# Full attention layers in another order beside the causal layers, and causal score matmuls of 512 columns

## The chip, the cores and the metric

The kernel runs on one NeuronCore of one Trainium2 chip. The metric is the device time of one execution in microseconds; below, "time" is the median over several executions. TensorE is called PE, its weight loads PEld, VectorE DVE, ScalarE ACT, GpSimd POOL, SyncE SP.

## What is computed

Four layers follow each other on a batch of B = 4 images with C = 256 channels and N = 32 x 32 = 1024 positions, all in float32:

```python
x = L0(x)   # q, k of 32 channels, v of 256; softmax(q k) v; gamma * out + x
x = L1(x)   # group norm; q, k, v of 256 channels; softmax(q k / 16) v; wo; + x
x = L2(x)   # causal: layer norm, 8 heads of 32 with one common k and v,
            # softmax(causal(q k)) v, wo; layer norm; feed-forward with
            # two layer norms and gelu; tokens x channels
x = L3(x)   # as L1, with weights of its own
```

L0, L1 and L3 are full attention: for each image 1024 x 1024 scores, a softmax over a row and the product with the values. L2 is causal multi-query attention over the same 1024 positions, with a feed-forward part behind it. Images don't depend on each other; in one image the layers do.

## The kernel before

**Two streams.** All work is cut into pieces. One stream, the full stream (`full_chain`), runs the twelve full layers (a layer on an image, as L1.3 for layer L1 on image 3) one after the other in the order of the list `FULL` (line 35). The other, the causal stream (`causal_chain`), runs the causal layer L2 on image 0, 1, 2, 3, named C0 to C3. A string for each engine (`ORDER`, line 43) says from which stream its next piece comes: `weave` (line 270) takes one character after the other and lets that stream emit one piece. For PE the character is also the PSUM bank at which the piece's output begins (0 to 7 for the full stream, a to h for the causal), F and C where a piece opens no new output. There are 1317 PE pieces, 690 of ACT, 868 of DVE, 128 of POOL and 66 of SP. All is fixed when the kernel is built; at run time engines wait for each other by semaphores, and each works through its pieces in order.

**Full layer.** `full_events` (line 97) lists its PE pieces: group norm means `gn` (L1, L3), queries `q`, values `v`, then for each of eight tiles of 128 positions the scores `s` (two steps of 512 keys), transposes of the normalised probabilities `t` (two steps), and for each quarter of the positions the value product `o` (four steps of eight matmuls, line 732). A full layer has 54 (L0) or 56 steps. ACT takes the exponent (line 1036) and copies transposes (1049); DVE takes row maxima, scales and adds the residual.

**Causal layer.** An image has 162 PE steps. For each of K = 8 blocks (a group of four heads by a quarter of 256 queries) there are `max` steps (`causal_max`, line 933: scores queries x keys, from which DVE takes the row maximum, line 1565), a `shift` step that turns the maxima, `exp` steps (`causal_exponents`, line 951: scores keys x queries, for the tile jt of 128 keys, with the shift as two more rows of the contraction; ACT takes the exponent, line 1205) and `values` steps (line 978). The queries of four heads lie in `qs` [128, 2, 4, 512]: four slices of 512 columns. Outputs for the four heads stand side by side in one or two banks of 512 columns (`heads`, line 545; `width` says how many banks). Then come, for each quarter, `wo`, layer norms, `ta`, `w1`, `tg`, `w2`, each of which needs the one before it. In `max` the causal mask of a diagonal tile is added by a bf16 matmul of 128 columns (line 948) right after each score matmul (line 946). In `exp` each head is a matmul of its own (line 959), with the same stationary operand:

```python
for a in range(4):
    last = mm(heads(name)[:, a, 0:n], ks[0:3 * DH + 2, jt * P:(jt + 1) * P],
              stack(k, a, 3 * DH + 2, QUARTER - n, QUARTER), start=True, stop=True)
```

n is 256 queries, or 128 for the second tile on the diagonal; of the 160 `exp` steps of the kernel 128 have n = 256 and 32 have n = 128.

**Buffers.** `home` (line 369) says where a layer's image lies: L0 and L1 in x[b % 2], L3 in z (image 3: in x[0]). x[0] and x[1] are loaded by SP once the causal layer has read their former image. The output of L2 goes to L3's home; as z is used for three images in turn, PE waits (in `stage`, kind w2) for the stores of the image before to be done. Group norm statistics of L3 have one buffer. SP carries all DMAs in order: the x loads, the stores of L3's results (`stores`, line 579), the copies that build `qs` (`stacks`, 586) and those of the shifts (`shifts`, 601).

Of the kernel before, what the change touches and what calls it, by code (L numbers as in the profile page):

```python
# [34 lines left out]
FULL = [("L0", 0), ("L1", 0), ("L0", 1), ("L1", 1), ("L0", 2), ("L3", 0), ("L1", 2), ("L0", 3), ("L3", 1), ("L1", 3),  # L35
# [14 lines left out]
        "FhdFbCFfd0chF6e23e0b2FFF630FFF6aCCeCgC1adfFdCfd3bC3fa2aFhe5aFc0cC52hfa2CFhC560FcfC725Fahca7C23eaFgcFeFag4CFa"  # L50
        "g360heCF37C6eFCFaCFhC3fF017fC5dC6FaFhFcf4C6aC2FdFFeCaC2F4gCFC0Cc3fF0F62FCe015F723Fab025FFghF3F60Cbb3F576FaFF"
        "2F745ag0b2FFF37geha6hFhFFceagc3eahcea6Fc3adf6a3FfCga2FhefC0cheC5c3a5caFC4c3a5aFdC27fab3Fhf6h05bCcFaCFceFagC2"
        "eaFge5a62ahF567FFF2F01567FFF320FFF5hCCbCdC5hacFaCcaaCcaaehc5aeC20FgfcCeC0fcCegcFeCcgeabgdCfb135hdCCbCeC6bCFf"
        "43bC6FeCb3e01gFfC3g0C6fFbCFaFChC5CFCh3c40F5Cg72FFF3Fa1256h4FFdaF12Cf7FFFda25dhF02e5F0F2hega4h4g0F2df7dfabd5F"
# [21 lines left out]
    "POOL": (
        "FCCCCCCCCCCCCCCFCCCCCCCCCCCCCCCCCCFCCCCCCCCCCCFCCCCCCCCCCCCCCCCCCCCCFCCCCCCCCCFCCCCCCCCCCCCCCCCCCFCCCCCCCCCC"
        "CCCCCCCCCCCCCCCCCCCF"),
    "SP": (
        "FCCCCCCCCCCCCCCFCCCCCCCCCFCCCFCCCCCCCCCCCCCCFFCCCCCCCCCCCFCCCCFCFF"),  # L80
# [1585 lines left out]
```

## Time and profile before

| what | value |
|---|---|
| time, median of 3 executions | 1485.58 us (1484.95 to 1488.01) |
| the profiled execution, its own time | 1486.03 us |
| its span, first to last instruction | 1484.2 us |
| instructions | 22513, of them 9152 matmuls and as many weight loads |
| mean granted TensorE clock | 0.958 of full speed |
| DMA | 27.09 MB, 18 GB/s |

The profile tells for each engine how long it was busy, and for each group of instructions (a line of the kernel, an operation, a tile) how often and how long one ran, and what ended the idle time before it. A matmul's duration reaches from its start to the modelled end of its pipeline; matmuls overlap, so the pace of a series is the distance of their starts. The granted clock is the share of its full speed that TensorE was given; it has two levels, 1.2 and 2.4 GHz (0.5 and 1).

### The profile page before, as it was taken

What the parts mean: (1) busy time and instruction counts of PE and PEld (TensorE: products, weight loads), DVE (VectorE), ACT (ScalarE), POOL (GpSimd) and SP (SyncE); (2) the same over time, 40 slices, a digit from 0 to 9 for tenths busy, and PEclk for the clock granted to TensorE, in tenths of its full rate; (3) what the DMA queues carried; (4) which work ended last, traced back from release to release, by engine and by line L of the source; (5) the groups of instructions that cost most, each with busy time, mean ns of one, the idle gap of its engine ahead of it and who ended that gap; (6) DMA issues with size and microseconds to landing.
All of it is one profiled execution on the core that took longest, in us unless ns stands there. A gap on an engine that the chain in (4) does not pass through costs nothing.

```text
span 1484.2 us, 22513 instructions
## 1 busy us (share of the span) xinstructions
PE 1338.0 (90%) x9152; PEld 1067.9 (72%) x9152; DVE 870.6 (59%) x1854; ACT 595.3 (40%) x973; POOL 92.5 (6%) x134
## 2 busy tenths in 40 slices
PE   5889989999999899989997899988999899998498
PEld 5768766777778777767776777776678777765486
DVE  3634466776458567557456657727656667675442
ACT  3523334344355343435334534423544443444142
POOL 0000000000000000000000000000010001001000
PEclk9999989999999899999998999997999999999699
DMA  5000010000000200010000010010000100100000
GB/s 176 1 1 0 29 43 23 1 23 2 1 1 2 70 11 14 22 29 1 2 1 0 6 38 23 2 49 3 1 2 1 43 2 23 37 16 1 0 1 29
DMA packets 20613, 27.09 MB, mean 18 GB/s; under 512 B 3488, under 2 KB 14240, under 8 KB 20512
## 3 DMA queue, kind: packets, MB, share of 16 engines
q1 hardware_dynamic: 20512, 25.66, 6.2%
q8 instruction: 74, 1.21, 0.3%
q14 instruction: 27, 0.22, 0.1%
HBM read 8.61 MB, written 4.19 MB: 9 GB/s over the span
## 4 chain that ended last, share of the span: by engine, by line
PE 79%; DVE 9%; ACT 6%; issue 2%; DMA 1%; SPq 1%; POOL 0%; ACTq 0%; DVEq 0%
PE ring L679 27%; PE ring L732 22%; PE ring L978 9%; PE ring L946 5%; PE ring L959 5%; PE ring L723 4%; ACT probs L1036 2%; PE ring L760 1%; PE ring L881 1%; ACT probsT L1049 1%; ACT cprobs L1205 1%; PE ring L948 1%; PE ring L916 1%; DVE part_max L1565 1%; SPq L595 1%
## 5 line engine op out<-in xcount | busy, mean ns | idle before, releaser
L732 PE MATMUL ring<-probsT,vt 128*128 128x256 f32 x1536 | 358.5, 387 | 16.7 <-ACT probsT L1049 16.4
L732 PEld LDWEIGHTS ring<-probsT,vt 128*128 128x128 f32 x1536 | 288.6, 193 | 67.4 <-ACT probsT L1049 20.6
L1205 ACT ACTIVATE cprobs<-ring 128x1024 f32<-128x1024 f32 (+1 forms) x160 | 150.4, 942 | 247.6 <-PE ring L959 246.9
L1036 ACT ACTIVATE probs<-ring,neg_max 128x1024 f32<-128x1024 f32 x96 | 107.1, 1116 | 185.4 <-DVE neg_max L1282 87.7
L1565 DVE TENSOR_REDUCE part_max<-ring 128x2 f32<-128x1024 f32 (+2 forms) x112 | 127.2, 1143 | 47.6 <-PE ring L946 34.2
L946 PE MATMUL ring<-ks,qs 96*128 96x512 f32 (+3 forms) x384 | 129.8, 421 | 16.4 <-ACT cprobs L1205 3.7
L1049 ACT COPY probsT<-ring 128x512 f32<-128x512 f32 x192 | 102.3, 592 | 48.2 <-PE ring L723 48.2
L959 PE MATMUL ring<-qs,ks 98*128 98x256 f32 (+1 forms) x640 | 114.5, 302 | 5.8 <-ACT probs L1036 1.4
L1281 DVE TENSOR_REDUCE shift_max<-ring 128x1 f32<-128x1024 f32 x64 | 78.3, 1224 | 70.3 <-PE ring L679 68.4
L723 PE MATMUL ring<-consts,probs 128*128 128x128 f32 x768 | 106.7, 279 | 13.1 <-ACT probs L1036 7.3
L959 PEld LDWEIGHTS ring<-qs,ks 98*128 98x128 f32 x640 | 91.4, 192 | 27.4 <-issue 15.6
L723 PEld LDWEIGHTS ring<-consts,probs 128*128 128x128 f32 x768 | 88.0, 143 | 32.1 <-ACT probs L1036 8.5
L679 PE MATMUL ring<-h_hi,q_hi 128*128 128x512 f32 x256 | 106.5, 416 | 3.6 <-ACT probs L1036 3.2
L946 PEld LDWEIGHTS ring<-ks,qs 96*128 96x128 f32 x384 | 77.4, 211 | 34.6 <-issue 10.4
L679 PE MATMUL ring<-h_hi,q_lo 128*128 128x512 f32 x256 | 100.5, 392 | 0.0
L679 PE MATMUL ring<-h_lo,q_hi 128*128 128x512 f32 x256 | 100.2, 392 | 0.0
L978 PE MATMUL ring<-cprobs,v 128*32 128x256 f32 (+1 forms) x1280 | 96.9, 375 | 0.0
L978 PE MATMUL ring<-cprobs,ones 128*32 128x256 f32 (+1 forms) x1280 | 92.9, 362 | 0.0
L643 POOL TENSOR_TENSOR rstd<-var_eps,half_neg 128x2 f32<-128x2 f32 (+1 forms) x56 | 44.8, 801 | 538.2 <-DVE var_eps L1463 538.2
L658 POOL TENSOR_SCALAR_AFFINE_SELECT cprobs<-cprobs 128x512 f32<-128x512 f32 x64 | 41.9, 657 | 540.6 <-ACT cprobs L1205 540.5
L1293 DVE TENSOR_SCALAR probs<-probs,row_inv 128x1024 f32<-128x1024 f32 x96 | 72.4, 754 | 3.4
L679 PEld LDWEIGHTS ring<-h_hi,q_hi 128*128 128x128 f32 x256 | 48.2, 188 | 19.9 <-issue 7.9
(215 smaller groups left out, 2212.1 us busy)
## 6 DMA issues: line engine op xcount, KB each, us to landing
x<-x_dram SPq DMA_DIRECT2D x4, 1024.0 KB, 6.5
qs<-q_hi SPq DMA_DIRECT2D x32, 128.0 KB, 2.3
qs<-q_hi SPq DMA_DIRECT2D x64, 64.0 KB, 2.0
out_dram<-z SPq DMA_DIRECT2D x6, 512.0 KB, 2.8
qs<-q_lo SPq DMA_DIRECT2D x16, 128.0 KB, 2.3
qs<-max_rows SPq DMA_DIRECT2D x128, 2.0 KB
qs<-q_lo SPq DMA_DIRECT2D x32, 64.0 KB, 2.0
out_dram<-x SPq DMA_DIRECT2D x2, 512.0 KB, 2.8
```

The source lines that it names most:

```text
L679: ins = mm(out, w, m, start=first and n == 0, stop=last and n == len(every) - 1)
L723: last = nc.tensor.transpose(o[:, j, :], probs[:, ti % 2, (TPH * hf + j) * P:(TPH * hf + j + 1) * P], ident)
L732: last = mm(o[:, ct * QUARTER:(ct + 1) * QUARTER], vt[:, j, ct * P:(ct + 1) * P], probsT[:, qi % (NQ - 1), j, :], start=j == 0, stop=j == ...
L946: last = mm(o, stack(k, a, 3 * DH, at, at + P), ks[0:3 * DH, lo:hi], start=True, stop=not diag)
L959: last = mm(heads(name)[:, a, 0:n], ks[0:3 * DH + 2, jt * P:(jt + 1) * P], stack(k, a, 3 * DH + 2, QUARTER - n, QUARTER), start=True, stop ...
L978: last = mm(acc[DH * a:DH * (a + 1), (half + 1) * QUARTER - n:(half + 1) * QUARTER], w, causal_probs(step, n)[:, a, :], start=jt == 0 and ...
L1036: A(probs[:, ti % 2, :], flat(full_name(l, b, ("s", ti))), ACT.Exp, bias=neg_max[:, ti:ti + 1], accum_out=row_sum[:, ti:ti + 1]).then_inc( ...
L1049: nc.scalar.copy(probsT[:, ti // 2 % (NQ - 1), js, (ti % 2) * P:(ti % 2 + 1) * P], slot(name)[:, 0, :].rearrange("p (s n) -> p s n", n=P)) ...
L1205: A(causal_probs(step, n), heads(name)[:, :, 0:n], ACT.Exp).then_inc(read_done["c", "act"], 1)
L1281: full_then(v.tensor_reduce(shift_max[:, ti:ti + 1], flat(name), AX_X, ALU.max, negate=True))
L1293: v.tensor_scalar(probs[:, ti % 2, :], probs[:, ti % 2, :], row_inv[:, ti:ti + 1], None, ALU.mult).then_inc(probs_scaled["dve"], 1)
L1565: v.tensor_reduce(cols if ti < TPH else parts[:, ch, :], src[:, :, 0:n], AX_X, ALU.max, negate=True).then_inc(read_done["c", "dve"], 1)
```

## The change

Three things. (1) In `FULL`, L1.3 stands before L3.1. (2) All five order strings are new; the numbers of pieces are the same. (3) In `causal_exponents` a matmul takes all heads that share a bank: two of 256 columns or four of 128; in `causal_max` the masks come after all scores of the tile, and only the first matmul of a bank has start=True, only the last stop=True.

With them, `home` gives L3.1 the buffer x[1], L3.2 x[0], L3.3 z, and L0.3 z; the x load of L0.3 moves behind the stores of L3.0 on SP and waits for them to be done; PE's wait for the stores goes; L3's statistics have two buffers.

```diff
-FULL = [("L0", 0), ("L1", 0), ("L0", 1), ("L1", 1), ("L0", 2), ("L3", 0), ("L1", 2), ("L0", 3), ("L3", 1), ("L1", 3),
+FULL = [("L0", 0), ("L1", 0), ("L0", 1), ("L1", 1), ("L0", 2), ("L3", 0), ("L1", 2), ("L0", 3), ("L1", 3), ("L3", 1),
         ("L3", 2), ("L3", 3)]
...
     "PE": (
-        "0F2eF60F2Fe50F72d5F401F756FFF3F750F62d7FFF0F6572d4FFF017FFF05F204F6F2046F012F405F710FFF2F456F012FFF3Ff70120F"
+        "0Fc4F60F2Fe50F72d5F401F760FFF3F516F021FFF3F0215ga1FFF027FFF03F513F5F0246F012F405F710FFF2F456F012FFF3F5670b3F"
...
     "SP": (
-        "FCCCCCCCCCCCCCCFCCCCCCCCCFCCCFCCCCCCCCCCCCCCFFCCCCCCCCCCCFCCCCFCFF"),
+        "FCCCCCCCCCCCCCCCCCCCCCCCCCCFCFFCCCCCCCCCCCCCCCCCCCCCCCFCCCFCCCFFFF"),
...
+        def gn_stats(l, b):
+            return all_stats[l][:, b % 2 if l == "L3" else 0, :, :, :]
+
         def home(l, b):
-            return x[b % 2] if l != "L3" else x[0] if b == B - 1 else z
+            return (z, x[1], x[0], z)[b] if l == "L3" else (x[0], x[1], x[0], z)[b]
...
             def full_chain():
-                for b in range(2, B):
-                    wait_filled(sp, f"C{b - 2}.xt1")
-                    sp.dma_start(home("L0", b)[:, :, :], x_dram[b]).then_inc(x_in[b % 2], 16)
-                    yield
-                for b in range(B):
+                wait_filled(sp, "C0.xt1")
+                sp.dma_start(home("L0", 2)[:, :, :], x_dram[2]).then_inc(x_in[0], 16)
+                yield
+                yield from stores(0)
+                sp.wait_ge(y_out, 16 * NB)
+                sp.dma_start(home("L0", 3)[:, :, :], x_dram[3]).then_inc(x_in[1], 16)
+                yield
+                for b in range(1, B):
                     yield from stores(b)
...
                 elif kind == "w2":
-                    if 0 < b < B - 1 and hf == 0:
-                        pe.wait_ge(y_out, 16 * NB * b)
...
-                for i in range(4) if two == 2 else range(2):
-                    o = heads(name)[:, i, 0:hi - lo] if two == 2 else slot(name)[:, i, 0:hi - lo]
+                own = 4 // width[name] if two == 2 else 1
+                outs = [(heads(name) if two == 2 else slot(name))[:, i, 0:hi - lo] for i in range(4 if two == 2 else 2)]
+                for i, o in enumerate(outs):
                     a = i if two == 2 else 2 * two + i
-                    last = mm(o, stack(k, a, 3 * DH, at, at + P), ks[0:3 * DH, lo:hi], start=True, stop=not diag)
-                    if diag:
-                        last = mm(o[:, hi - lo - P:hi - lo], mask[:, 0, :], mask[:, 1, :], start=False, stop=True)
+                    last = mm(o, stack(k, a, 3 * DH, at, at + P), ks[0:3 * DH, lo:hi], start=i % own == 0,
+                              stop=not diag and i % own == own - 1)
+                if diag:
+                    for i, o in enumerate(outs):
+                        last = mm(o[:, hi - lo - P:hi - lo], mask[:, 0, :], mask[:, 1, :], start=False,
+                                  stop=i % own == own - 1)
...
-                for a in range(4):
-                    last = mm(heads(name)[:, a, 0:n], ks[0:3 * DH + 2, jt * P:(jt + 1) * P],
-                              stack(k, a, 3 * DH + 2, QUARTER - n, QUARTER), start=True, stop=True)
+                own = 4 // width[name]
+                for a in range(0, 4, own):
+                    last = mm(heads(name)[:, a:a + own, 0:n], ks[0:3 * DH + 2, jt * P:(jt + 1) * P],
+                              stack(k, slice(a, a + own), 3 * DH + 2, QUARTER - n, QUARTER), start=True, stop=True)
```

What the new strings do, counted from the PE string (first and last step of each layer among the 1317):

| layer | before | changed |
|---|---|---|
| C0 | 101 to 425 | 105 to 402 |
| L0.1, L1.1 | 118 to 235, 246 to 366 | 118 to 230, 239 to 379 |
| C1 | 426 to 744 | 403 to 714 |
| L0.2, L3.0, L1.2 | 371 to 446, 447 to 569, 570 to 697 | 382 to 465, 473 to 603, 607 to 713 |
| C2 | 745 to 1038 | 715 to 991 |
| L0.3 | 702 to 780 | 717 to 821 |
| L3.1 | 786 to 897 | 983 to 1114 |
| L1.3 | 898 to 1043 | 841 to 981 |
| C3 | 1039 to 1260 | 992 to 1260 |
| L3.2 | 1046 to 1202 | 1123 to 1259 |
| L3.3 | 1261 to 1316 | 1261 to 1316 |

In the last steps of C3 (`tg2`, `w22`, `wo3`, `ta3`, `w13`, `tg3`, `w23`) no step of a full layer stands between them before. Changed, L3.2's `t10` to `t13` and two `o` steps stand between `wo3` and `ta3`, two `o` steps between `ta3` and `w13`, `t14`, `t15` and two `o` steps between `w13` and `tg3`, and two `o` steps between the two halves of `w23`.

## Rows read from the trace of the kernel before

**Rows 1.** The profile page: busy time of each engine, and the chain that ended last.
```profile
PE 1338.0 (90%) x9152; PEld 1067.9 (72%) x9152; DVE 870.6 (59%) x1854; ACT 595.3 (40%) x973; POOL 92.5 (6%) x134
...
PE 79%; DVE 9%; ACT 6%; issue 2%; DMA 1%; SPq 1%; POOL 0%; ACTq 0%; DVEq 0%
```

**Rows 2.** Windows: us, then busy us (x instructions) by engine, granted PE clock, DMA.
```profile
149.40:478.50 329.10, 308.63 (x2183) 244.63 (x2182) 210.31 (x431) 143.06 (x225) 22.16 (x31) 0.97 0.06 14
478.50:827.60 349.10, 320.95 (x2224) 255.54 (x2223) 209.85 (x446) 143.11 (x230) 22.83 (x32) 0.96 0.06 16
827.60:1150.40 322.80, 298.24 (x2087) 233.90 (x2086) 195.90 (x429) 132.01 (x216) 23.61 (x32) 0.96 0.06 14
1150.40:1321.90 171.50, 159.28 (x1150) 125.22 (x1149) 116.16 (x250) 68.74 (x112) 14.98 (x21) 0.98 0.09 23
1321.90:1402.10 80.20, 55.87 (x508) 40.20 (x506) 42.93 (x108) 28.15 (x40) 7.19 (x10) 0.83 0.02 8
```

**Rows 3.** Waits of PE from 1321.9 to 1402.1 us: total, times, longest.
```profile
PE ring L881 <- DVE an L1479: 12.2, 3, 6.9
PE ring L679 <- DVE act_lo L1544: 4.0, 2, 3.4
PE ring L902 <- DVE max_cols L1576: 3.0, 1, 3.0
```

**Rows 4.** PE in order of time before L3.3: start, us; idle before in brackets.
```profile
1385.37 1.11 PE L881 MATMUL ring<-consts,an 128*128 128x128 f32 x4 [6.88 <-DVE an L1479]
...
1387.90 0.58 PE L679 MATMUL ring<-ffw_hi,hn_hi 128*128 128x256 f32 x1 [1.41 <-DVE hn_lo L1249]
...
1394.43 1.11 PE L881 MATMUL ring<-consts,an 128*128 128x128 f32 x4 [3.61 <-DVE an L1479]
...
1402.13 0.39 PE L750 MATMUL ring<-gn_in,consts 128*128 128x4 f32 x2 [2.60 <-DVE gn_in L1326]
...
1406.12 0.77 PE L760 MATMUL ring<-h_hi,L_wqk_hi 128*128 128x512 f32 x1 [3.60 <-issue]
```

**Rows 5.** PE in order of time: scores in fours, and a value step.
```profile
1239.86 1.09 PE L946 MATMUL ring<-ks,qs 96*128 96x512 f32 x4
...
705.93 1.89 PE L732 MATMUL ring<-probsT,vt 128*128 128x256 f32 x8
```

**Rows 6.** Groups by form: busy us, mean ns of one; idle before.
```profile
L959 PE MATMUL ring<-qs,ks 98*128 98x256 f32 x512 | 93.7, 306 | 5.7 <-ACT probs L1036 1.4 <-DMA qs<-max_rows 1.4 <-DVE part_max L1565 1.1
L959 PE MATMUL ring<-qs,ks 98*128 98x128 f32 x128 | 20.8, 285 | 0.1
L959 PEld LDWEIGHTS ring<-qs,ks 98*128 98x128 f32 x640 | 91.4, 192 | 27.4 <-issue 15.6 <-DVE part_max L1565 1.8 <-DMA qs<-max_rows 1.6
L948 PEld LDWEIGHTS ring<-mask 128*128 128x128 bf16 x256 | 26.5, 104 | 21.6 <-issue 9.0
L679 PE MATMUL ring<-h_hi,q_lo 128*128 128x512 f32 x256 | 100.5, 392 | 0.0
...
ACT cprobs L1205 <- PE ring L959: 246.9, 112, 8.3
```

**Rows 7.** PE in order of time: score and mask by turns, 384 and 512 columns.
```profile
1202.37 0.44 PE L946 MATMUL ring<-ks,qs 96*128 96x384 f32 x1 [1.29 <-DVE h_lo L1249]
...
1202.69 0.42 PE L946 MATMUL ring<-ks,qs 96*128 96x384 f32 x1
...
1203.47 0.45 PE L946 MATMUL ring<-ks,qs 96*128 96x512 f32 x1
...
1203.80 0.47 PE L946 MATMUL ring<-ks,qs 96*128 96x512 f32 x1
```

**Rows 8.** Waits of PE over the span, and DMA issues (to landing).
```profile
PE ring L916 <- DMA out_dram<-z: 3.3, 2, 1.7
...
x<-x_dram SPq DMA_DIRECT2D x4, 1024.0 KB, 6.5
...
out_dram<-z SPq DMA_DIRECT2D x6, 512.0 KB, 2.8
```

More of the change, by code:

```diff
@@ L50 @@
[L50 to L54, printed above, removed]
@@ new lines @@
+        "FF457FFFac4F6F0ce5F0F2h4F670F234gFahc601hFaFF4cgacFg7a6c0F457gcFcaefFcaFf1F3705gCgbegbCdhaC6fbdFaCfFcaFcCe76"
+        "h6aFfFhabCceCbFhdfCbgda6fb1F3hfCC1dC6fCFb2eFgeC6bddC1fa3ahc5dFa7dC05hbFd7C03bCFfa7C56dhaFdCFadFahfc0cCFec624"
+        "dFdCC6a23CeCFgCFaFbC3fCFac75a6d4C7aCFgFdCFaC76fC3CFCeFcFCa6F3F15F3Fh0c5F730FecCfd725F017FdFF5F20db3Fh156FFF2"
+        "F701efec70bFhFFfcaeh67c6aFFhecaheFcaeaCbg0hgcCehaC1adFf3dCa5dfdC1F5dFh0ceh5c0dC4gFaC360Feh36ehC4aFgc0b67ecFF"
+        "agCFC4cCFa7C62aF04f7fFcCeFcFcCe6acFef0123g4acFCgFhFa2C4dC4FgaFCFcga4gCca4F6ca6e1gFdC5Fbd3hfC1C3gC1dFC76f3CFb"
@@ new lines @@
+        "275FdCb7C34acFfhFCFaC3fF7a6C0FdC576aCFCCFhfF1FCa34706FhFFh017FgfFFCca6F4F2a6F4F2ah4F620Fd764F076bcaeFhFhF1F0"
+        "7dfdfbca4F76da2aedgFaeFfF0F7eCcf34cf6aCchaC5FFgbdFaCg2d2adC2FfhFaFdedcCfaCecgaCebgdea2hgCCe0FC6cC4a6beFaC4aF"
+        "ggCe0cgef6ca6aC2Fega74C0gCFc74cC2aeFgaC4g5a6cheFacCFeaF2egCCaFCeC60b4CgFc6C01eCcgFeFhCcCFa4bCFaCh3C72C0Cbf7F"
+        "FFCg707FFFg7a3Fcb53Cfc0F4F6c04ch0Fc345F701F340fgbcFFbFh4F0cg1cgeca5Fhcace7aca10fFFhCdbF4agbCFahgC6320be6ceCa"
+        "bFdbCFFdha52dhgaC7ebCdaFbfCdFafcdaFgfCCdChC0bf3Fa5aC5d0fFdC5Facch0ge2ac4C0hcF75dCcC3F750Fc475cCaeFcaCFcageca"
@@ new lines @@
+        "gCaFc6F23abCCaCfChCacCfCahc4F601cCdCafCcCaCFCCagFF4FCh63271FaFFa760FbcFFC74F026F4F0264F012F704F617FFF2F014F6"
+        "73FFF0F27657FFF017FFF"),
+    "ACT": (
+        "FFFFCFFFFFCCFFFCCFFFCCFFFFFFFFFFFFFFCCFFFFFFFFFFFFFFFFFFFFFFFFFFFFFFFFCFFFFCCFFFCCFFFFFFFFFFFFCCCCCFFFCCFFFC"
+        "CCCFCCFFFFCCCCCCCFFCCCCCCCCCCFFFFCCFCCFCFFCCFCFCCFFFCCFFFCCFFFCCCCCCCFFFCCFFFCCCCCCFFFFFCCCCCFFFFCCCCFFFCFFF"
+        "CFFFCCCFFFFFFCCCFFFFFFFFFFFCCCCCFFCCCCCCCCFFCCCCCFFFCCFCFFCCFFCCFFFCCFFFCCFFFCCCCCFFFCFFFCCCCFFFFFCCCFFCCCCC"
+        "FFCFFFCFCFFCCFFCCFFFCFFFCCCFFFCCCCCFFFCFFFCCCCFFFFFCFFFFCCCCFFFCFFFCCFFFFFFFFFCCCCFFFCCCFFFCCCCCCFFFCCCCFFCF"
+        "CFCCCCCCCCCCCCCFFCFFCFCFCFCFCCFCFCCFFFCCFFFCCCFFFCCCCCCCFFCFCFFFCCCCCCCCCFFFFFCCCFFCFFFCFFCCCFCFFFFCCFFFFFFF"
+        "FFCCCCFFFCCCCCFFFCCCCCCCCFFFCFFCCCCFCFCCCCCCCCCCCCFFFFFCCFCFCFFCFCCFFFCFFFCFFFCCCCCCCCFCCCFFCCCCCFFCFCCCCCCC"
+        "FFFFFCFFCCFFFFFFFFFFFFFFFFFFFFFFFFFFFFFFFF"),
@@ new lines @@
+    "DVE": (
+        "CFFFFCFFFFFFCCFFCCFFCCCFFFFFFFFFFFCCFFFFFFFFFFFFFFFFFFFFFFFFFFFFFFCCCFFFFCCFCCFCCFFFCFFFFCFFCCCFFFFCCCCCFFFC"
+        "CCCFCFFFCCCCCCCCCCCCCCCCCFCCCCCFCCCCCCCCFCFFCFCFCFFCCCFFCCFCCCFCFCCCCCFCCCFCCCCFCCCFCFCFCFCFCCCCFCCCCCCCFFFC"
+        "FCFCCCCCFCCCFCCCCCFCCCCFFFCCCCFCCCFCFFCFCCFCFCFFCCCFFCCCFCCFFFCCFCFFFFFCCCCFFFCCCCCCCCCCFFFFCFCCCCCCCFFCFCCC"
+        "CCCCFCCCCFCFCFFCCCCCCFCFFCFCCFCFCCFCCCFCFFCFCCCFCCCCCFCCCCFCCFCCCCCFCCCFFCFCFCFFFCFCCCCFCCFCFFFCFFFCCFCFCCCF"
+        "CCCCCFCFCFCFFCCCCFFCCCCFCCCCCFCCCCFFFCCCFCCCFCCFFFFCCFCFFFFFCCCCFFFCCCCCFFFCCCCCFFFCCCCCFCCCCCCCCCCCCFCCCCCF"
+        "FCCCCCCCCCCFCFCCCCFFCFFFCFCCCCCCFCCFFCCCCCFCCCCCCFCFCFCFCFCFCCCFCCCCCCCFCFFCFCCFCCCCCCCCFCCCFFCCCCFCCCCCCCCF"
+        "FCFFCCFCFFFCCCCFCCCFCCFFFCCFCFFFFCFCCCFFCCCCCFFCCCCFCCFCCCCCCCFCCCFCCCCCCCCCCCFCCCCCCCCCCCCCCCFFCCFCFCFFCFCF"
+        "CCCCCFCCFCCFCCFCCCCFCFCFCFFFFCCCCCCCCCCCCFFCFCCCCCCFCCCCCFCCCCCCCFFCCCCFCCCCCFCCCCFCFFFFFFFFFFFFFFFFFFFFFFFF"
@@ L75 @@
         "FFFF"),
     "POOL": (
[L77 to L78 removed]
+        "FCCCCCCCCCCCCCFCCCCCCCCCCCCCCCCCCCCCCCFCCCCCCCCCCCCCCFCCCCCCCCCCCCCCCCCCCCCCCFCCCCCCCCCCCCCCCCFCCCCCCCCCCCCC"
+        "CCCFCCCCCCCCCCCCCCCF"),
     "SP": (
[L80 removed]
+        "FCCCCCCCCCCCCCCCCCCCCCCCCCCFCFFCCCCCCCCCCCCCCCCCCCCCCCFCCCFCCCFFFF"),
```

33 lines of the change are left out of this document (5 added, 28 removed).

## The prediction, made before the changed kernel was run

> **What bounds the kernel now.** I read the page first, then the busy time by stage, then the waits and the order of time where the stages differ. The page shows a kernel that is bound by TensorE: PE is busy in 90% of the span and carries 79% of the chain that ended last; the other engines stand at 59% and below [rows 1]. So two things can shorten it: less time on PE for the same work, and fewer holes in PE's stream. The windows say where the holes are [rows 2]. Each of the first three causal images (149.4 to 478.5, 478.5 to 827.6, 827.6 to 1150.4 us) keeps PE busy for 308.6 of 329.1, 320.9 of 349.1 and 298.2 of 322.8 us: 94, 92 and 92%. The last causal image runs at 93% (159.3 of 171.5 us) while the full layer L3.2 runs beside it. When L3.2 has ended, at 1321.9 us, 80.2 us follow in which the causal image is alone; there PE is busy for only 55.9 us and its granted clock is 0.83 of full speed, where 0.98 was granted just before. PE waits in that stretch for the layer norms of the feed-forward part: 12.2 us in three waits for the normalised rows `an`, 4.0 for `act_lo`, 3.0 for `max_cols` [rows 3]. In order of time one sees the last pieces hand over serially: a gap of 6.88 us, one of 1.41, one of 3.61, then 2.60 and 3.60 us at the group norm of L3.3 [rows 4].
>
> **Cover for the lonely tail.** Steps of PE, counted in the order string: before, the last causal image has 162 steps of its own and 60 of full layers beside it, the last of which stands 58 steps ahead of the image's end. Changed, L1.3 comes before L3.1, so that image 3 of the causal layer starts with L3.1 and L3.2 both still to do: 107 full steps beside it, and L3.2's last value step is the second last step of the stage. Between the causal pieces `wo3`, `ta3`, `w13`, `tg3`, `w23` now stand transposes and value products of L3.2 (six, two, four and two steps in a row; a value step is eight matmuls in 1.89 us [rows 5]), which is about what the gaps of rows 4 last. Price: PE's 55.9 busy us were done at clock 0.83; at 0.98 they are 55.9 x 0.83/0.98 = 47.3, and at the 93% busy of the stretch before, 50.9 us. The 80.2 us become 50.9: **29.3 us gained**. The gaps of 2.60 and 3.60 us at the end stay: L3.3's group norm still needs the last `w2`, and nothing is left to cover it.
>
> **The cover is taken from somewhere.** The other three images have 163, 157 and 132 full steps beside them and will have 136, 150 and 115. Does a stage with fewer full steps run thinner? The rows say hardly: the stretch 1150.4 to 1321.9, with 60 full steps for 104 causal ones, is as dense (93%) as the first image with one full step per causal step (94%). I take 5 us for it, half a point of busy share on the 1001 us of those stages; bounds 0 and 29, the latter if all that the tail lost turns up again.
>
> **Exponent matmuls merged.** For 256 queries the four matmuls of 256 columns become two of 512, for 128 queries four become one of 512. 512 matmuls of 256 columns were busy 93.7 us in 128 groups of four, 732 ns a group; with a mean of 306 ns for one, their starts are (732-306)/3 = 142 ns apart. For 128 columns: 20.8 us in 32 groups, 650 ns, starts (650-285)/3 = 122 ns apart [rows 6]. Matmuls of 512 columns of the same kind, four in 1.09 us whose last takes some 0.39 [rows 5, 6], start (1.09-0.39)/3 = 233 ns apart. So a large piece goes from 4 x 142 = 568 to 467 ns, 128 times: 12.9 us; a small one from 4 x 122 = 488 to 233 ns, 32 times: 8.2 us. Together **21 us of PE**. The multiplied columns are the same: what goes are 352 of the 640 weight loads of 192 ns [rows 6], of which matmuls of 256 columns (half of 233 ns, 117) leave 25 ns each in sight, and short ones more.
> The Trainium skill ("TensorE: Matmul & The Clock Gate", "Back-to-back issue gap" and "Step-by-step") speaks against this part: it has the isolated gap as N/2.4 + 2.5 ns and lets the next weight load be pulled under the matmul in flight, by which a large piece would gain 5 ns and nearly the whole 21 us would not be there, while the 142 ns of this trace say otherwise. The measurement decides for me.
>
> **Score matmuls for the maximum.** Same count, but the masks come after all scores of a tile instead of after each. A score of 512 columns and its mask start 330 ns apart from the next pair, one of 384 columns 320 ns [rows 7]; streaming alone is 233 + 58 and 175 + 58 (scaled from the 233). There are 256 pairs. The lower bound is zero, if a mask behind a mask takes its 104 ns of weight load [rows 6]: 233 + 104 is no less than 330. The upper bound is some 65 ns a pair, 16 us. I take 5, nearer to the load's row.
>
> **What of this reaches the end.** PE is in order and 90% busy; a gain ahead of a wait is swallowed by it. Of 21 + 5 us I count nine tenths: **23.4 us**.
>
> **Buffers and queues.** The output of the causal image 1 now goes to the second x buffer instead of z, and PE's wait for the stores ahead of `w2` goes away: 3.3 us in two waits [rows 8], **3.3 us gained**. In its place SyncE waits for L3.0's two stores before it loads x for L0.3. That load takes 6.5 us and a store 2.8 [rows 8]; it is issued about 115 PE steps ahead of L0.3's first matmul (1317 steps in 1484 us, so over 120 us): hidden. If it weren't, its 9.3 us would show once at L0.3's start. Behind that wait on SyncE stand the copy of the last shift of image 1 (`shift7`, whose transposes come 26 PE steps, nearly 30 us, later), then image 2: hidden too. The doubled statistics buffer, and GpSimd's order with the same 128 steps, cost nothing: same instructions, on engines at 59% and 6%. What cover there is goes with PE's backlog; without it the group norm's chain on DVE and GpSimd would show, 6.2 us a layer as at L3.3 [rows 4].
>
> **Sum.** The profiled execution took 1486.0 us, its span 1484.2. 1486.0 - 29.3 + 5 - 23.4 - 3.3 = 1435.0. That run lies 0.4 us above the median of the three; I leave it at **1435 us**. Its own range is 1416 (masks at 16, merges in full, nothing lost from the other stages) to 1449.
>
> **Rivals.**
> *Merges swallowed* (0.16): PE's saved time ends in waits that end on ACT or DVE, or the weight loads were hidden anyway. For it: ACT waited for the exponent scores for 246.9 us in all [rows 8], so it is not the bound there, but 15% of the chain that ended last is DVE's and ACT's [rows 1]. Against: 90% busy and 142 ns. Then 1435 + 23.4 = 1458 us. The rule of the Trainium skill's page on TensorE quoted above would come out here too.
> *The holes move* (0.17): the three earlier images, with 51 full steps fewer, open the holes that closed at the end. For it: 24.3 us of idle PE over 58 lonely steps is 0.4 us a step, and 51 steps make 21 us. Against: the density of rows 2. Then the 29.3 come back in place of the 5: 1459 us. Both together (0.03) is 1483 us, no change.
> *Slower* (0.05): the merged matmul reads two or four head slices that lie 512 columns apart; if such a moving operand streamed at half rate, 512 columns would take 467 ns, a large piece 933, so 128 x 365 = 46.7 us more instead of 12.9 less, and the small ones 0.7 less instead of 8.2. 1435 + 19 (the gain missing) + 41.4 (nine tenths of 46.0) = 1495 us. It decides from about 420 ns a matmul. No row shows such an operand on PE; none hints at a cost either.
> *Not what it says* (0.01 of the above): the words speak of four full layers left; by the list three are left behind L1.3, of which two run beside the causal image and L3.3 after it. I reckon with the two.
>
> **Numbers.** Forecast 0.59, merges swallowed 0.16, holes move 0.17, both 0.03, slower 0.05. What a measurement of this kernel can tell is about 0.2%, 3 us. Faster 0.92, same 0.03, slower 0.05. The range runs from 1416, where all bounds meet, to 1467, past both middle rivals; what it leaves out is the slower case, the two rivals together, and a little on either side.
>
> **What would show it.** Right: `L959` with 288 matmuls and starts 233 ns apart, some 9,150 - 352 = 8,800 matmuls; PE's busy time down by 20 us or more beyond what the clock gives; the last 80 us ahead of L3.3's group norm over 90% busy at a clock above 0.95; no wait of PE on stores; gaps only at the last group norm. Wrong: a busy share under 90% in the first three images (holes moved); ACT's or DVE's waits at those images up by as much as PE's work went down (swallowed); matmuls of `L959` 400 ns apart (slower).

## The result, and the profile after

| | before | changed |
|---|---|---|
| time, median | 1485.26 us (1484.59 to 1488.01, 4 runs) | **1416.6 us** (1414.86 to 1420.27, 4 runs) |
| ratio | | **0.9538**, 95% interval 0.9514 to 0.9561 |
| profiled execution, its span | 1486.03, 1484.2 us | 1414.86, 1413.1 us |
| mean granted TensorE clock | 0.958 | 0.973 |

The change took 68.7 us; 51 were forecast (1435 us). The time lies at the low end of the range. Times below are medians over executions; one of e1's ten executions (2067.94 us, mean clock 0.602) and one of e3's five (1727.27 us, 0.735) are left out, and with them the medians would be 1483.2 and 1478.7 us, the latter being the figure from which the expectations of e6 and e9 start. The page of the changed kernel, busy time and chain, against [rows 1], and the merged group from its section 5 (busy us, mean ns):

```profile
PE 1303.7 (92%) x8800; PEld 1018.9 (72%) x8800; DVE 866.2 (61%) x1854; ACT 594.1 (42%) x973; POOL 93.9 (7%) x134
...
PE 82%; DVE 7%; ACT 7%; issue 2%; SPq 1%; DMA 1%; POOL 0%; ACTq 0%; DVEq 0%
...
L968 PE MATMUL ring<-qs,ks 98*128 98x512 f32 x288 | 106.6, 442 | 4.9 <-DVE h_lo L1258 2.4
```

The counts are those of the forecast: 8800 matmuls, 288 of them merged. PE's busy time fell by 34.3 us. The idle part of the span (span less busy) fell from 146 to 109 us. The matmul edits account for some 14 us of the 34.3 (e1 and e2 below). The rest goes with the clock: by the mean clocks of the table PE stood at half clock for about 125 us before (2 x (1 - 0.958) x 1484.2) and 76 after. A matmul of 512 columns starts 0.43 us behind the one before it at half clock (L3.3's queries, 1335.25 to 1335.68 us) and 0.23 at full, so this is worth at most 24 us, an estimate from those two rows. e4 below, with the new order and the old matmuls, shows it by itself: the same 9152 matmuls, busy for 19.6 us less than before, at a mean clock of 0.972.

```profile
PE 1318.4 (93%) x9152; PEld 1055.7 (74%) x9152; DVE 867.5 (61%) x1854; ACT 594.3 (42%) x973; POOL 94.2 (7%) x134
```

So three kinds of gain are there: fewer holes, more of the span at full clock, and less work on PE.

The windows of the changed kernel, for the same five stages as [rows 2] (us, then busy us by engine, clock, DMA); the last is that of the last 58 causal steps, up to L3.3:

```profile
148.90:456.20 307.30, 283.77 (x1976) 217.49 (x1975) 195.00 (x408) 134.97 (x209) 21.96 (x31) 0.97 0.06 15
456.20:775.80 319.60, 302.72 (x2091) 235.13 (x2090) 203.84 (x443) 137.30 (x227) 22.93 (x32) 0.99 0.07 18
775.80:1054.90 279.10, 259.10 (x1854) 196.28 (x1853) 189.77 (x412) 122.33 (x196) 24.33 (x32) 0.97 0.05 13
1054.90:1234.80 179.90, 171.33 (x1177) 131.65 (x1176) 126.04 (x268) 77.72 (x130) 15.77 (x21) 0.98 0.10 25
1234.80:1330.50 95.70, 89.63 (x686) 67.64 (x684) 54.69 (x131) 41.41 (x63) 7.19 (x10) 0.98 0.03 12
```

The last 58 causal steps now share their stretch with the end of L3.2: PE is busy for 89.6 of 95.7 us (94%) at clock 0.98, where it was busy for 55.9 of 80.2 (70%) at 0.83. The first three images run at 92, 95 and 93%, where they ran at 94, 92 and 92%, with 27, 7 and 17 full steps fewer beside them: the first is slightly thinner (23.5 idle us instead of 20.5), the other two are not, and the second has 16.9 idle us instead of 28.2. None of the waits of [rows 3] is left in the last stretch. These are all waits of PE that the profile lists from 1235 to 1331 us (the second belongs to L3.3), and the gaps in order of time that answer to [rows 4]:

```profile
PE ring L738 <- ACT probsT L1058: 3.4, 2, 2.7
PE ring L756 <- DVE gn_in L1334: 2.6, 1, 2.6
```

```profile
1330.50 0.59 PE L756 MATMUL ring<-gn_in,consts 128*128 128x4 f32 x2 [2.60 <-DVE gn_in L1334]
...
1334.69 0.76 PE L766 MATMUL ring<-h_hi,L_wqk_hi 128*128 128x512 f32 x1 [3.60 <-issue]
```

The 2.60 and 3.60 us at L3.3's group norm are there unchanged, as forecast. No wait of PE for stores is left in the whole span.

### The profile page after: what moved, and what is told of

The parts are those of the page before. It is cut to its first block, busy times and chain, and to the rows that moved or that the text cites. A ratio compares the mean times of both kernels' runs of the same rounds, so it can differ in the third digit from the quotient of the medians.

```text
span 1413.1 us, 21791 instructions
## 1 busy us (share of the span) xinstructions
PE 1303.7 (92%) x8800; PEld 1018.9 (72%) x8800; DVE 866.2 (61%) x1854; ACT 594.1 (42%) x973; POOL 93.9 (7%) x134
## 4 chain that ended last, share of the span: by engine, by line
PE 82%; DVE 7%; ACT 7%; issue 2%; SPq 1%; DMA 1%; POOL 0%; ACTq 0%; DVEq 0%
PE ring L685 26%; PE ring L738 25%; PE ring L987 9%; PE ring L951 5%; PE ring L968 5%; PE ring L729 4%; ACT probs L1045 2%; ACT probsT L1058 1%; PE ring L766 1%; PE ring L887 1%; ACT cprobs L1214 1%; DVE part_max L1573 1%; PE ring L955 1%; PE ring L920 1%; PE ring L772 1%
## 5 line engine op out<-in xcount | busy, mean ns | idle before, releaser
L738 PE MATMUL ring<-probsT,vt 128*128 128x256 f32 x1536 | 363.3, 387 | 16.9 <-ACT probsT L1058 16.0
L951 PE MATMUL ring<-ks,qs 96*128 96x512 f32 (+3 forms) x384 | 111.2, 388 | 13.8 <-ACT cprobs L1214 5.0
L968 PE MATMUL ring<-qs,ks 98*128 98x512 f32 x288 | 106.6, 442 | 4.9 <-DVE h_lo L1258 2.4
L951 PEld LDWEIGHTS ring<-ks,qs 96*128 96x128 f32 x384 | 63.4, 197 | 37.3 <-issue 9.8
L1594 DVE RECIPROCAL sums<-sums 128x128 f32<-128x128 f32 x64 | 57.8, 930 | 21.8 <-ACT nums L1223 21.5
L968 PEld LDWEIGHTS ring<-qs,ks 98*128 98x128 f32 x288 | 49.6, 192 | 25.9 <-issue 13.9
```

The lines of the kernel that those rows point to most:

```text
L738: last = mm(o[:, ct * QUARTER:(ct + 1) * QUARTER], vt[:, j, ct * P:(ct + 1) * P], probsT[:, qi % (NQ - 1), j, :], start=j == 0, stop=j == ...
L951: last = mm(o, stack(k, a, 3 * DH, at, at + P), ks[0:3 * DH, lo:hi], start=i % own == 0, stop=not diag and i % own == own - 1)
L968: last = mm(heads(name)[:, a:a + own, 0:n], ks[0:3 * DH + 2, jt * P:(jt + 1) * P], stack(k, slice(a, a + own), 3 * DH + 2, QUARTER - n, QU ...
```

## The experiments

Eleven kernels. Each comparison is with runs of the kernel before on the same chip, whose medians were 1485.39 (e1 to e4), 1485.13 (e5 to e8) and 1484.87 us (e9 to e11).

### The matmul edits alone: e1, e2, e3, e4

e1 puts the merged exponent matmuls into the kernel before, e2 the masks behind the scores, e3 both; e4 is the changed kernel with both taken out.

```diff
+                own = 4 // width[name]
-                for a in range(4):
-                    last = mm(heads(name)[:, a, 0:n], ks[0:3 * DH + 2, jt * P:(jt + 1) * P],
-                              stack(k, a, 3 * DH + 2, QUARTER - n, QUARTER), start=True, stop=True)
+                for a in range(0, 4, own):
+                    last = mm(heads(name)[:, a:a + own, 0:n], ks[0:3 * DH + 2, jt * P:(jt + 1) * P],
+                              stack(k, slice(a, a + own), 3 * DH + 2, QUARTER - n, QUARTER), start=True, stop=True)
```

> The kernel before with one edit: the exponent scores merged to 512 columns (two matmuls for 256 queries, one for 128), old order. By the prediction's term: 21 us of PE, nine tenths of it seen, so about 1466 us (ratio 0.987). Rival, by the trace of the changed kernel: inside a piece of 256 queries the four matmuls already started 0.12 us apart, so a piece loses only some 15 ns of streaming plus what its first load costs; the pieces of 128 queries go from 0.49 to 0.32 us. Then 128 x 0.04 + 32 x 0.2, about 12 us: 1474 us. If these scores are always waited for elsewhere: 1485 us, no change.

Measured: 1482.6 us, ratio 0.9978 (0.996 to 0.9995). That is 2.8 us instead of 19, and less than the 12 of the rival in the expectation, too. The two pieces side by side show why. Before, in order of time (start, us), a large and a small piece, each with its successor on PE:

```profile
689.81 0.56 PE L959 MATMUL ring<-qs,ks 98*128 98x128 f32 x4
690.30 0.64 PE L978 MATMUL ring<-cprobs,v 128*32 128x256 f32 x8
...
694.99 0.64 PE L959 MATMUL ring<-qs,ks 98*128 98x256 f32 x4
695.47 0.63 PE L946 MATMUL ring<-ks,qs 96*128 96x512 f32 x2
```

Changed:

```profile
691.03 0.63 PE L968 MATMUL ring<-qs,ks 98*128 98x512 f32 x2
691.50 0.40 PE L685 MATMUL ring<-h_hi,q_hi 128*128 128x512 f32 x1
...
694.82 0.48 PE L968 MATMUL ring<-qs,ks 98*128 98x512 f32 x1
695.13 0.40 PE L685 MATMUL ring<-h_hi,q_hi 128*128 128x512 f32 x1
```

A large piece holds PE for 0.48 us before and 0.47 merged: its four matmuls of 256 columns already started 0.12 us apart, (0.64 - 0.28)/3, which is their streaming time (half of 233 ns), so the loads, though recorded with 192 ns each, were wholly hidden inside the piece. Only the small pieces gain, from 0.49 to 0.31 us: there the starts stood (0.56 - 0.28)/3 = 0.09 us apart on the mean (0.06, 0.11 and 0.11 in this piece), where 128 columns stream in 0.058, so part of each load was in sight. Summed over the trace from the start of a piece to the start of its successor, e1's large pieces take 98.4 us against 98.5 and the small ones 14.6 against 19.6, waits of PE included; without the waits it is 78.9 against 79.5 and 12.8 against 18.0.

For e2 (and e3) the edit of `causal_max`:

```diff
-                    last = mm(o, stack(k, a, 3 * DH, at, at + P), ks[0:3 * DH, lo:hi], start=True, stop=not diag)
-                    if diag:
-                        last = mm(o[:, hi - lo - P:hi - lo], mask[:, 0, :], mask[:, 1, :], start=False, stop=True)
+                    last = mm(o, stack(k, a, 3 * DH, at, at + P), ks[0:3 * DH, lo:hi], start=i % own == 0,
+                              stop=not diag and i % own == own - 1)
+                if diag:
+                    for i, o in enumerate(outs):
+                        last = mm(o[:, hi - lo - P:hi - lo], mask[:, 0, :], mask[:, 1, :], start=False,
+                                  stop=i % own == own - 1)
```

> The kernel before with one edit: in the score tiles for the maximum the causal masks follow all scores of the tile, old order. By the prediction's term: 5 us, seen as 4 to 5, about 1481 us. Rival, by the trace of the changed kernel, where a tile of four scores and four masks took 0.79 us at the median against 1.00 and one of two and two 0.66 against 0.70: some 12 us, 1474 us. Zero if a mask behind a mask is held by its own weight load.

Measured: 1480.7 us, ratio 0.9964 (0.9944 to 0.9984), 4.7 us. The steps of `causal_max`, from the start of each series to the start of what follows it on PE, took 144.3 us instead of 152.6, waits included. The groups of e2 that answer to the masks (busy us, mean ns; the masks were busy 60.9 us before):

```profile
L951 PE MATMUL ring<-mask 128*128 128x128 bf16 x256 | 33.4, 237 | 0.0
...
L951 PEld LDWEIGHTS ring<-mask 128*128 128x128 bf16 x256 | 16.1, 106 | 14.8 <-issue 13.8
```

and four masks in a row in the changed kernel:

```profile
1152.55 0.40 PE L955 MATMUL ring<-mask 128*128 128x128 bf16 x4
```

They start (0.40 - 0.23)/3 = 0.06 us apart. A mask behind a mask isn't held by its 104 ns of weight load, which was my lower bound.

> The kernel before with both matmul edits, old order. Prediction: 26 us of PE, nine tenths of it seen: 1462 us. Swallowed: above 1475 us. If the two edits add up with the rival sizes of the two runs before: 1461 to 1465 us as well, with the parts the other way round.

Measured: 1476.7 us, ratio 0.9933 (0.9905 to 0.996): 8.7 us, where e1 and e2 together make 7.5. Only four executions count here, from 1469.1 to 1478.8 us, so this figure is good to some 4 us.

e4 is the changed kernel with the two diffs above reversed:

```diff
-                own = 4 // width[name]
-                for a in range(0, 4, own):
+                for a in range(4):
```

> The changed kernel with both matmul edits undone: new order and buffers, old matmuls. If order and matmuls add up, this is 1416.6 plus what they save, 23 to 26 us: 1440 us, and the order with the buffers is worth 45 us, against the 27.6 us (29.3 - 5 + 3.3) of the prediction. If the new order only pays together with the shorter pieces it was searched for, it is well above, 1455 us.

Measured: 1428.61 us, ratio 0.963 (0.9607 to 0.9654). So **order and buffers alone give 57 us**, twice what I had counted for them (29.3 + 3.3 - 5 = 27.6), and the matmul edits give 12.0 us on top in the new order, about half of 23.4.

### The buffers alone: e5

The new homes, the second statistics buffer, SP's new order and no wait of PE for stores, all else as before:

```diff
-            return x[b % 2] if l != "L3" else x[0] if b == B - 1 else z
+            return (z, x[1], x[0], z)[b] if l == "L3" else (x[0], x[1], x[0], z)[b]
...
-                    if 0 < b < B - 1 and hf == 0:
-                        pe.wait_ge(y_out, 16 * NB * b)
```

> The kernel before with the buffers of the changed one alone: L3.1 in the second x buffer, L3.2 in the first, L3.3 and the x of L0.3 in z, that load behind L3.0's stores, no wait of PE for stores. Old order, old matmuls. Prediction's term: the 3.3 us of two waits go, 1482 us. Rival: the causal pieces queued behind are waited for anyway, 1485 us.

Measured: 1482.62 us, ratio 0.9981 (0.997 to 0.9992): 2.5 us, near the 3.3 forecast.

### The tail: e6, e7

e7 is the changed kernel with L3.2 done before the last 58 causal steps, as it was before; e6 is e3 with L3.2's end, from its first value step on, woven into these steps as in the changed kernel. Each diff shows the first changed line of PE's string; the lines behind it, and ACT's, DVE's and (e6) SP's strings, follow it.

```diff
-        "bFdbCFFdha52dhgaC7ebCdaFbfCdFafcdaFgfCCdChC0bf3Fa5aC5d0fFdC5Facch0ge2ac4C0hcF75dCcC3F750Fc475cCaeFcaCFcageca"
+        "bFdbCFFdha52dhgaC7ebCdaFbfCdFafcdaFgfCCdChC0bf3Fa5aC5d0fFdC5Facch0ge2ac4C0hcF75dCcC3F750F234FFF0F752F401FFF2"
```

> The changed kernel, but all of L3.2 is done before the last 58 causal steps, which stand alone as before the change. Cover theory: the tail is 25 to 29 us longer, 1443 us, and the rest of the gain stays. If the order's gain lies elsewhere (at the joints of the layers): under 10 us more, 1425 us.

Measured: 1449.7 us, ratio 0.9757 (0.973 to 0.9784): the cover of the tail is worth **33.1 us**, where 29.3 were forecast. The two profiled executions say somewhat less: the stages from the last image to L3.3 take 304.1 us in e7 and 275.6 in the changed kernel, 28.5 us apart. e7's was 10.6 us behind when they began, though both kernels have the same pieces in the same order up to there. The last two windows of e7 ahead of L3.3, and its longest waits of PE in the second:

```profile
1065.50:1289.80 224.30, 212.98 (x1389) 167.69 (x1387) 138.25 (x290) 88.70 (x150) 15.74 (x21) 0.98 0.08 20
1289.80:1369.60 79.80, 55.16 (x474) 36.39 (x472) 42.98 (x108) 28.15 (x40) 7.18 (x10) 0.85 0.04 14
```

```profile
PE ring L892 <- DVE an L1492: 12.2, 3, 6.8
PE ring L690 <- DVE act_lo L1557: 4.0, 2, 3.4
```

The bare tail of [rows 2] and [rows 3] is back, almost to the tenth. And the full steps moved out of it didn't fill anything: the stage ahead grew by 44.4 us (179.9 to 224.3), at 95% busy as before, so nothing there had waited for cover.

```diff
-        "70bcbeagbd4gF12dCg0eFbhcCegbCFFhceaCh2FeaeC67cga4Fh3ghcC60ebCFdgbfCdFFbgfda6F4dcCCaCdC0bc674FFacCgaFcCa5g5cg"
+        "70bcbeagbd4gF12dCgdhafCbdeChfaeCcgaeCgcaefdgCbeCgabeCfacheagcCCdCfCabdfCaceCacfehacfCeabCdCf4aCcfFacCFfachfa"
```

> Old order of the layers with both matmul edits (1478.7 us without this), but the last 32 steps of the full layer L3.2 (from its first value step on) are held back and woven into the last 58 causal steps as in the changed kernel. Cover theory: the 80 us tail fills, and what it gains is near the 25 to 29 us of the prediction: 1452 us. Rival, the holes move: the earlier part of the last image, left with 24 full steps for 104 causal ones, opens as much, 1475 us.

Measured: 1473.73 us, ratio 0.9919 (0.9899 to 0.9939): 3.0 us less than e3, not 25, and with intervals that overlap, so it isn't shown that weaving alone gains anything. The same two windows, of e3 and of e6, and the three longest waits of PE in e6's first:

```profile
1139.70:1309.80 170.10, 157.66 (x1096) 120.50 (x1095) 116.25 (x250) 68.70 (x112) 14.76 (x21) 0.97 0.09 23
1309.80:1390.90 81.10, 56.19 (x475) 37.38 (x473) 42.84 (x108) 28.13 (x40) 7.18 (x10) 0.83 0.02 7
```

```profile
1145.20:1297.90 152.70, 125.53 (x892) 88.07 (x890) 106.53 (x232) 60.42 (x96) 14.31 (x21) 0.91 0.09 22
1297.90:1392.80 94.90, 88.86 (x680) 67.00 (x676) 52.23 (x126) 38.98 (x58) 7.62 (x11) 0.98 0.03 12
```

```profile
PE ring L907 <- DVE max_cols L1586: 7.1, 3, 3.2
PE ring L765 <- issue: 4.7, 1, 4.7
PE ring L952 <- issue: 3.6, 1, 3.6
```

The tail is filled as in the changed kernel (94% at 0.98), and the stage ahead of it opens: idle 12.4 to 27.2 us, clock 0.97 to 0.91. The holes moved, though not to the images of my rival but to the stage right ahead. My reading is that the cover needs the exchange of L1.3 and L3.1, which puts 47 more full steps beside the last image. This is argued and not shown: the exchange alone was not run, and in e6 the stage ahead of the tail was not searched anew for its 32 missing steps.

### The banks: e8

A control, since new strings also change the PSUM banks: the changed kernel, for its last 148 PE steps with banks chosen by the rule "free for longest" instead. One of the two lines:

```diff
-        "gCaFc6F23abCCaCfChCacCfCahc4F601cCdCafCcCaCFCCagFF4FCh63271FaFFa760FbcFFC74F026F4F0264F012F704F617FFF2F014F6"
+        "gCaFd6F01fdCCeCgCdCefCaCdhf0F234fCaCgcCaCfCFCCgcFF0FCd57640FbFFc357FgeFFC12F503F6F1460F324F670F324FFF5F701F3"
```

> Control for the two runs before: the changed kernel with the same order, PSUM banks of the last 148 steps given out by the same simple rule that those two use (the banks free longest). If the rule costs nothing: 1416.6 us within 3. If it costs: up to 5 us more, and as much is to be taken off the other two.

Measured: 1415.92 us, ratio 0.9531 (0.9517 to 0.9545): no difference, and e6 and e7, whose banks were chosen by that rule, are compared fairly.

### The other images: e9

e7's tail is bare and it stands 27.0 us below e3 (1476.7), 24.5 without the buffers. In the profiled executions (2.0 us below and 4.0 above their medians) the tail begins at 1309.8 us in e3 and at 1289.8 in e7. In the four stages ahead of it PE is idle for 87.1 and 71.5 us; the other 4.4 us of these 20.0 are busy time of PE. The first and the third image, of e3 and then of e7:

```profile
148.50:473.00 324.50, 303.50 (x2095) 234.28 (x2094) 210.22 (x431) 142.78 (x225) 21.88 (x31) 0.98 0.05 14
819.80:1139.70 319.90, 294.76 (x1999) 223.33 (x1998) 195.78 (x429) 131.83 (x216) 23.62 (x32) 0.96 0.06 14
```

```profile
148.60:461.90 313.30, 289.94 (x2004) 223.39 (x2003) 198.59 (x414) 135.70 (x210) 21.92 (x31) 0.96 0.06 15
786.10:1065.50 279.40, 259.03 (x1855) 196.24 (x1854) 189.83 (x412) 122.33 (x196) 24.30 (x32) 0.97 0.05 13
```

Most of the difference in idle time lies in the second image; its window and its longest waits of PE, of e3:

```profile
473.00:819.80 346.80, 318.23 (x2135) 247.66 (x2134) 209.57 (x446) 143.26 (x230) 22.71 (x32) 0.96 0.06 16
```

```profile
PE ring L732 <- ACT probsT L1054: 5.0, 3, 3.3
PE ring L750 <- DVE gn_in L1331: 4.4, 2, 2.6
PE ring L723 <- ACT probs L1041: 3.6, 1, 3.6
```

and of e7:

```profile
461.90:786.10 324.20, 307.78 (x2090) 238.94 (x2089) 203.09 (x442) 137.12 (x225) 23.18 (x32) 0.97 0.06 17
```

```profile
PE ring L743 <- ACT probsT L1063: 3.4, 2, 2.7
PE ring L690 <- ACT cprobs L1219: 2.1, 2, 1.1
...
PE ring L761 <- DVE gn_in L1339: 0.4, 1, 0.4
```

At two joints between full layers PE waits for a group norm in e3, at none for long in e7. e9 tests whether these joints are the cause: e3 with the new buffers, and at L3.0, L1.2 and L1.3 a few causal steps moved ahead of the layer's `gn`. One of three places in PE's string:

```diff
-        "17dFFF56ac7FgFF0hdfb6afF3bdgafc4g0Fcdfahceg0cF4gCca63fcaCg3fFcC01c6Fd01c6aCF4d20FFgdbCgdFe1hgFa345hCFb7dC12f"
+        "17dFFF56ac7FgFFhdfb06afF3bdgafc4g0Fcdfahceg0cF4gCca63fcaCg3fFcC01c6Fd01c6aCF4d20FFgdbCgdFe1hgFa345hCFb7dC12f"
```

> Old order of the layers with both matmul edits and the new buffers; one change in the order: at three joints where PE had nothing to do between the last value step of a layer and the group means of the next (gaps of 2.64, 1.74 and 1.73 us before L3.0, L1.2 and L1.3, and behind two of them 1.65 us for the stores), the causal steps that followed the group means now stand ahead of them (four score tiles, two halves of w2, two halves of w2). Joint theory: 1478.7 - 2.5 (buffers) - about 5 of idle and 2 of clock: 1469 us. Rival: the group norm's chain of DVE and GpSimd is merely started later, 1476 us.

Measured: 1481.43 us in ten runs from 1465.87 to 1483.88, ratio 0.9954 (0.9928 to 0.998). Its interval overlaps that of e3 (0.9905 to 0.996), so no gain is shown; at like clocks the two are alike (1472.34 and 1474.76 us at 0.958). The trace shows what became of the joints. The waits there did shrink: over the whole span PE waits 5.2 us for `gn_in` instead of e3's 11.4, and no longer for stores (3.3). But others took their place, 6.1 us for `heads_out_lo` among them, which e3 doesn't have at all. The second and the third image of e9 have 55.0 idle us, those of e3 53.7:

```profile
471.00:818.40 347.40, 315.37 (x2135) 245.02 (x2134) 209.45 (x446) 142.93 (x230) 22.92 (x32) 0.96 0.06 16
818.40:1130.80 312.40, 289.40 (x1999) 220.10 (x1998) 195.58 (x429) 131.56 (x216) 23.74 (x32) 0.98 0.06 15
```

Moving single steps at three joints doesn't bring what the new order brings.

### The clock: e10, e11

Both run matmuls of 512 columns whose results nothing uses, to fill PE's waits: e10 in the changed kernel at the group norms of L1.0 and L3.3, e11 in e7's bare tail, ahead of `shift7`, `ta3` and `tg3` (10, 26 and 13).

```diff
+            def warm(name, count):
+                w, m = wv0[0][:, 0, 0:P], wv0[0][:, :, :].rearrange("p c o -> p (c o)")
+                for _ in range(count):
+                    mm(slot(name)[:, 0, :], w, m, start=True, stop=True)
...
+                o = open_unit(full_name(l, b, ("gn", 0)))
+                if (l, b) in (("L1", 0), ("L3", 3)):
+                    warm(full_name(l, b, ("gn", 0)), 9)
                 pe.wait_ge(gn_in_ready, n)
-                o = open_unit(full_name(l, b, ("gn", 0)))
...
+                o = open_unit(full_name(l, b, ("q", 0)))
+                if (l, b) in (("L1", 0), ("L3", 3)):
+                    warm(full_name(l, b, ("q", 0)), 13)
                 pe.wait_ge(h_hi, 2 * n + 1)
-                o = open_unit(full_name(l, b, ("q", 0)))
```

> The changed kernel with idle PE time filled at the two group norms that nothing covers (L1.0 and L3.3): 9 matmuls of 512 columns into the group means' own bank ahead of them, 13 into the queries' own bank ahead of those; they compute nothing that is kept. The gaps there (2.64 and 3.6 us) are not shortened; what is at stake is the granted clock after them, at half for 6.9 us at L1.0 and 10.2 us at L3.3. Clock theory: up to half of these 17 us back, 1409 us. Rival: the clock falls for another reason, or the dummies delay the norm: 1417 us or more.

Measured: 1416.07 us, ratio 0.9532 (0.9511 to 0.9553): no change in the time. Yet the clock is kept. The stretch behind L3.3's norm, changed kernel and then e10:

```profile
1327.00:1345.00 18.00, 11.80 (x54) 10.08 (x53) 8.66 (x24) 7.26 (x13) 0.69 (x1) 0.72 0.08 30
```

```profile
1327.90:1345.00 17.10, 16.10 (x87) 13.37 (x86) 9.15 (x24) 7.63 (x13) 0.70 (x1) 1.00 0.09 32
```

From L3.3's first query step to PE's last instruction it took 71.8 us instead of 74.3. What these 2.5 us became is seen in the profiled run alone: in its second image PE stood at half clock for 19.5 us, against 6.8 in the changed kernel's, and the stage took 324.5 instead of 319.6 us. Over the whole profiled execution the fill took only some 6 us off the time at half clock (77.6 to 71.5). Four runs of each don't tell 2.5 us apart from such a shift.

> The changed kernel with the bare tail (1449.7 us), and idle PE time in it filled with matmuls of 512 columns that compute nothing kept: 10 ahead of shift7, 26 ahead of ta3, 13 ahead of tg3. The waits stay; 23.9 of the 79.8 us of the tail were at half clock. Clock theory: PE work in the tail runs at full clock, some 8 us back, 1441 us; then the bare tail costs about 25 us of waits and 8 of clock. Rival: the chain of layer norms sets the pace and PE's clock does not matter: 1449 us.

Measured: 1447.81 us, ratio 0.9753 (0.9727 to 0.9779), 1.9 us below e7 with intervals that overlap. Its tail:

```profile
1282.30:1359.60 77.30, 63.56 (x524) 42.98 (x522) 43.03 (x108) 28.15 (x40) 7.18 (x10) 0.93 0.04 15
```

The clock rose from 0.85 to 0.93 and the tail shrank by 2.5 of 79.8 us. The time at half clock in it fell from 23.9 to 10.2 us, and 2.5 us came of it. So the bare tail is not long mainly because its clock is low: most of it is the serial hand-overs between PE, DVE and ACT, and the low clock comes with them. A tail wholly at full clock was not run.

## Why the prediction was right and where it was not

The sum, part by part. The measured values are differences of medians; the last row is what is left of the 68.7.

| part | forecast | measured |
|---|---|---|
| tail covered | -29.3 | -33.1 (e7 to the changed kernel) |
| other images | +5 | -21.1 (the rest; 24.5 from e3 to e7) |
| matmul edits | -23.4 | -12.0 in the new order (e4), -8.7 in the old (e3) |
| buffers | -3.3 | -2.5 (e5) |
| together | -51.0 | -68.7 |

**Cover for the lonely tail: right.** Place, mechanism and size: the waits of [rows 3] are gone, the stretch runs at 94% and 0.98, 33 us by the medians (28.5 between the profiled executions) against 29.3. The gaps at L3.3's norm stayed.

**The cover is taken from somewhere: wrong in sign.** I argued from density that a stage with fewer full steps runs hardly thinner. Where steps were taken, that nearly held: the first image, with 27 fewer, went from 94 to 92%. But I priced the new order only by how many full steps stand beside each image, and this count says nothing of where they stand. The windows show the second image with 16.9 idle us instead of 28.2 and a clock of 0.99 instead of 0.96, and the fourth stage at 95% instead of 93%. The step that failed is that the new strings' worth outside the tail was put at a loss from 0 to 29 us, with no gain as its other end. e7 against e3 shows a gain of 24.5 us there; between their profiled runs it is 20.0, of which idle PE is 15.6 (87.1 to 71.5). The sum also priced the clock in the tail alone, and left it at nothing elsewhere: in the four stages ahead of it PE stood at half clock for some 78 us before the change and for 51 after it. Part of that is chance, as e7, with the order of the changed kernel up to its last image, has 68 there. Which places in the order bring the gain stays open: the joints' waits are shorter in e7's second image, but e9, which filled three joints, only moved them. I didn't try to exchange L1.3 and L3.1 alone, with the rest of the old order kept.

**Exponent matmuls merged: mis-sized, 21 us of PE where 5 were there.** The step that failed is "their starts are (732-306)/3 = 142 ns apart" for [rows 6]. I read a mean over 128 groups as the pace inside a piece. Busy time in a group of rows also holds pieces run at half clock and the first interval, in which the load stands in sight. The rows in order of time were there to be read: (0.64 - 0.28)/3 = 0.12 us. With it a large piece has 4 x 117 = 468 ns against 2 x 233 = 466, so no gain; the small ones gain, 5 us instead of 8.2. The rule that I set aside (the Trainium skill, "TensorE: Matmul & The Clock Gate", "Back-to-back issue gap", with the weight load pulled under the matmul in flight as in "Step-by-step: what each phase is for") had the large pieces right: it gives 5 ns for one, and 0.01 us is what the two large pieces above show. For a small piece it would give 8 ns, an estimate from the same formula (4 x 55.8 against 215.8), and there the trace disagrees with 0.18 us (0.49 to 0.31). Its isolated gap for 512 columns is 216 ns; the trace has 233.

**Masks: under-sized, 5 where 8.3 us of PE went.** The lower bound rested on a load that would hold a mask behind a mask; four in a row start 0.06 us apart.

**What of this reaches the end: nine tenths was right in the new order.** 5 + 8.3 = 13.3 us less on PE gave 12.0 us there, and 8.7 in the old. Less in the old order would fit the forecast's own ground, that time saved ahead of a wait is lost in it, with 146 idle us in that span against 109; but e3's interval reaches from 6 to 14 us and holds both values, so the difference is not shown.

**Buffers: right**, 2.5 against 3.3; SP's later load shows nowhere.

**The rivals.** *Merges swallowed* came true for the larger part, for its second reason (loads hidden anyway) and not by waits on ACT: ACT's wait for the exponent scores is what it was, 246.9 us (a row of [rows 6]; the prediction points at [rows 8] for it), now

```profile
ACT cprobs L1214 <- PE ring L968: 247.7, 109, 6.7
```

*The holes move* fell for this order and held for weaving alone (e6), though they moved one stage up and not into the earlier images. *Slower* fell: two merged matmuls and their successor take 0.47 us, not 0.93, so a moving operand of two slices that lie apart streams at full pace. That 1416.6 lies within the range is partly luck: an unforeseen gain of 21 us, where a loss of 5 was counted, met a matmul term 11 us too large. The sum's own upper end, 1449 us, doesn't follow from its bounds: a loss of 29 us instead of 5 alone gives 1459.

## What to carry to other kernels

Look for the stretch where one stream runs alone and keep independent work for it, but see where that work is taken from: here weaving alone moved the holes one stage up (3 us, within the scatter), and with the layers exchanged and the order searched anew the same cover gave 33. Fewer holes also mean more time at full clock: with the matmuls unchanged, the new order left PE busy for 19.6 us less (e4). Before counting a gain from fewer, larger matmuls, read the distance of starts inside one piece in order of time; where it equals the streaming time, merging gains nothing, whatever duration is recorded for the weight loads. When an order is searched anew, put the unlisted places at a range with both signs; counting what stands beside what doesn't price them.

## What the runs showed of the hardware that was not expected

- **Where PE falls to half clock varies from run to run, and the time with it.** One and the same kernel, e9, took 1465.87 us at a mean clock of 0.962, 1474.77 at 0.957 and 1483.88 at 0.953; nine thousandths of the clock went with 18 us, 1.2%, of which the clock itself can make at most 13 (half of 2 x 0.009 x 1475 us, an estimate). The changed kernel and e7 have the same order in the first two images of the causal layer, and PE stood at half clock there for 27 us in the one profiled execution and 44 in the other. The changed kernel's four runs lie within 5.4 us.
- **Matmuls that compute nothing keep the clock at 1.00** through a norm of some 6 us (e10), and were worth 2.5 us in their stretch and nothing in the median.
- **bf16 matmuls of 128 columns behind one another start 0.06 us apart**, though the load of each is recorded with 106 ns in e2; by turns with float32 scores a pair took 320 to 330 ns [rows 7], where the streaming of both is 233 to 291.
